# A two-layer decoder on one core: the query and key projections of the last layer issued ahead of the scores in their slots on TensorE

## The reference

```python
q = apply_rotary_interleaved((query @ Wq).reshape(b, t, 2 * H, D), cos, sin)
k = apply_rotary_interleaved((query @ Wk).reshape(b, t, 2 * H, D), cos, sin)
s = jnp.where(mask, jnp.einsum('bthd,bshd->bhts', q, k) * scale, NEG)
a = jax.nn.softmax(s, axis=-1)          # for (q1, k1) and for (q2, k2)
attn_freq = rfft(attn1) - lambda_full * rfft(attn2)   # then a filter, irfft, rms norm, @ Wout
```

## Time and profile before

| | |
|---|---|
| median of 3 runs | 1355.0 us (1351.44 to 1356.1) |
| the profiled execution | 1357.66 us, span in the trace 1355.9 us |
| TensorE busy | 1122.7 us (83%) |
| VectorE busy | 918.3 us (68%) |
| ScalarE busy | 567.1 us (42%) |
| GpSimd busy | 539.5 us (40%) |
| mean granted TensorE clock | 0.915 |

### The profile page before, as it was taken

How to read it: one execution, slowest core, us unless ns; L and a number is a source line. 1 busy time by engine, 2 the same in 40 slices (tenths; PEclk the granted TensorE clock), 3 DMA queues, 4 the chain that set the end, 5 groups by cost and what they waited for, 6 DMA issues and landing times.

```text
span 1355.9 us, 25392 instructions
## 1 busy us (share of the span) xinstructions
PE 1122.7 (83%) x8338; PEld 960.4 (71%) x8338; DVE 918.3 (68%) x2195; ACT 567.1 (42%) x1998; POOL 539.5 (40%) x575
## 2 busy tenths in 40 slices
PE   6999999889899998966686999997588887788753
PEld 6898898888888888855575888885356655555532
DVE  5757778687877778687763557654367688787753
ACT  5533343333433242413242333332187776667631
POOL 1112222333424343343330556667134455563564
PEclk9999999999999999976897999998699898898876
DMA  5410010101010100106564777766200000000000
GB/s 169 133 65 23 1 41 1 61 14 56 18 49 22 39 27 19 47 30 190 157 198 146 144 143 116 116 113 84 70 17 9 24 17 24 16 17 9 16 24 16
DMA packets 72663, 84.13 MB, mean 62 GB/s; under 512 B 11720, under 2 KB 62632, under 8 KB 72408
## 3 DMA queue, kind: packets, MB, share of 16 engines
q1 hardware_dynamic: 55608, 60.74, 15.1%
q0 software_dynamic: 14592, 19.41, 8.5%
q10 hardware_dynamic: 2336, 2.36, 0.5%
HBM read 49.90 MB, written 32.58 MB: 61 GB/s over the span
## 4 chain that ended last, share of the span: by engine, by line
PE 38%; DVE 28%; DMA 12%; issue 9%; ACT 6%; POOL 5%; SPq 2%; DVEq 0%; POOLq 0%; ACTq 0%
PE bank L514 4%; PE bank L1987 4%; PE bank L515 4%; PE bank L516 4%; DMA yt<-y_sb,xe 3%; DMA xs<-xg,slot 3%; PE bank L575 3%; PE bank L1501 3%; DMA x_sh<-y_sb,xe 2%; PE bank L2000 2%; DVE at_lo L924 2%; DVE k_st L2295 2%; ACT ex L2119 2%; DMA xe<-xs 1%; PE bank L563 1%
## 5 line engine op out<-in xcount | busy, mean ns | idle before, releaser
L741 ACT ACTIVATE qk<-bank,b_col 128x256 f32<-128x256 f32 x256 | 107.1, 471 | 220.4 <-PE bank L516 218.0
L2119 ACT ACTIVATE ex<-bank,nmx 128x64 f32<-128x64 f32 x512 | 153.9, 353 | 70.8 <-DVE nmx L2304 63.8
L414 POOL TENSOR_TENSOR probs<-shifted,rowinv 64x512 f32<-64x512 f32 x64 | 71.0, 1109 | 276.4 <-DVE rowinv L912 209.7
L514 PE MATMUL bank<-xt_hi,w_hi 128*128 128x256 f32 x512 | 153.9, 301 | 5.3 <-DVE w_lo L876 4.9
L515 PE MATMUL bank<-xt_lo,w_hi 128*128 128x256 f32 x512 | 147.6, 288 | 0.0
L516 PE MATMUL bank<-xt_hi,w_lo 128*128 128x256 f32 x512 | 147.1, 287 | 0.0
L1885 POOL TENSOR_TENSOR k_bd<-k_st,bd_mask 128x512 f32<-128x512 f32 x64 | 69.7, 1094 | 153.0 <-PE bank L2000 136.2
L2119 ACT ACTIVATION_READ_ACCUMULATOR ex<-bank,nmx 128x1 f32 x512 | 123.0, 247 | 0.0
L757 ACT ACTIVATE at_hi<-bank,b_col 128x256 fp32r<-128x256 f32 x128 | 53.7, 471 | 134.2 <-PE bank L575 134.2
L1557 ACT ACTIVATE act_e<-bank 128x176 f32<-128x176 f32 x112 | 35.5, 317 | 173.4 <-PE bank L1447 173.4
L514 PEld LDWEIGHTS bank<-xt_hi,w_hi 128*128 128x128 f32 x512 | 101.2, 198 | 6.4 <-issue 4.5
(11 more groups left out here) (300 smaller groups left out, 3256.5 us busy)
## 6 DMA issues: line engine op xcount, KB each, us to landing
xe<-xs SPq DMA_DIRECT2D x80, 136.0 KB
e_stage<-w_up SPq DMA_DIRECT2D x18, 352.0 KB
terms<-w_qkv SPq DMA_DIRECT2D x12, 512.0 KB, 4.8
down<-w_down SPq DMA_DIRECT2D x16, 176.0 KB
xs<-zero SPq DMA_DIRECT2D x17, 136.0 KB, 2.5
yt<-zero ACTq DMA_DIRECT2D x1, 2176.0 KB, 8.3
xin<-x SPq DMA_DIRECT2D x8, 256.0 KB, 3.1
terms<-w_o SPq DMA_DIRECT2D x4, 512.0 KB, 4.8
```

Of the source, the lines that this page charges most:

```text
L414: pool.tensor_tensor(probs[r, :, SEQ * s:SEQ * s + SEQ], expd[r, :, :], rowinv[r, :].unsqueeze(2).broadcast_to([SEQ, TC * GH, SEQ]), ALU.m ...
L514: nc.tensor.matmul(out, l_hi, r_hi, start=start, stop=False, skip_group_check=True)
L741: ins = nc.scalar.activation(qk[:, par, hh, o, :], p_proj[hh % 2][:, o * TOK:o * TOK + TOK], ACT.Identity, bias=b_col[:, o, h:h + 1])
L2119: ins = nc.scalar.activation(ex[:, g % 2, j, :], p_s[g % 2][:, j * SEQ:j * SEQ + SEQ], ACT.Exp, bias=nmx[:, g % 2, j:j + 1], accum_out=rs[ ...
```

## The change

In slots 2 to 5 of the periods that prepare a block, `qk(t + 1, u - 2)` is issued between `pv(g - 3)` and `score(g + 2)`; before, it came behind the scores and behind `mix`, `xq_transpose` or `ffn`. Its instructions and its waits are the same, and no other engine's order is edited.

```diff
--- before.py
+++ after.py
@@ -2079,6 +2079,8 @@
                     turn_exp(g - 1)
                 if units(g - 3):
                     pv(g - 3)
+                if blocks(t + 1) and 2 <= u < 6:
+                    qk(t + 1, u - 2)
                 if units(g + 2):
                     score(g + 2)
                 if u == 0 and blocks(t - 2):
@@ -2096,8 +2098,6 @@
                         t1(t + 1)
                     if u == 1:
                         val(t + 1)
-                    if 2 <= u < 6:
-                        qk(t + 1, u - 2)
 
     def scalar_constants(act):
         def constants(r):
```

## The result

The changed kernel is slower: 1376.45 us as the median of 4 runs (1366.55 to 1380.99) beside 1353.22 us for the kernel before (4 runs), ratio 1.0137 with a 95% interval of 1.0094 to 1.018. A second measurement on another occasion gave 1.0148 (1.0109 to 1.0187). The forecast was 1369 in a range of 1357 to 1381.

A forecast was written before the change was run, and what follows sets the result against it. No engine is full; the last layer's period was taken as a ring of waits between engines working strictly in order. Order 8.9 us plus clock 5.1 gave 14 us, bringing the median from 1355.0 to 1369.0, range 1357 to 1381.

The forecast's parts named there:

- Slot 2 and the ring: Slot 2: scores behind qk0, maxima between projection and the rope freeing its bank; rope 2 at 8.25 us, loss 1.43.
- t=0: Period t=0, no rms or mix between: rope 4 at 17.31 us behind qk0, 13.83 before; cost 3.5 us.
- t=1 and 2: Periods t=1 and 2, mix covering the bank's freeing for qk2: rope 4 at 18.47 us; costs 1.9 and 1.5 us.
- the collision of k_st with GpSimd's sum: In t=2 GpSimd's sum moves to about 8.8 us and hits VectorE's k_st writes, giving 0.7 us back.
- the relief of the square: VectorE's rms square no longer runs beside GpSimd's k_bd, 0.69 instead of 1.41 us; 0.7 us taken off.
- rival (c): VectorE's small rms operations, at about 13.0 us, also wait for GpSimd's k_bd; 3 us more, 1372 us; chance 0.10.
- t=3 to 6: Periods t=3 to 6: rope 4 at 18.87 us behind qk0, 18.36 before; cost 0.5 us each, 2.0 for four.
- the lock's bound: VectorE and GpSimd blocking, t=3 to 6: -0.2 us with the square alone, +1.3 with k_st's collision and no relief.
- what delays the fourth rope delays the period: From the fourth rope VectorE is busy up to the period's last maxima, so the rope's delay passes to the period.
- rival (d): Tail of the period: VectorE alternating with GpSimd swallows the shift in t=1 to 6; only t=0 pays 3.5 us; chance 0.14.
- The clock: TensorE's gap before qk0 grows to 2.55 us; clock falls three times of seven at 1.7 us: 5.1 us, bounds 0 to 11.9.
- rival (b): TensorE's clock falls behind qk0's gap in every period: 1355 + 8.9 + 11.9 = 1376 us; chance 0.08.

The follow-up runs named there:

- experiment 3: The changed kernel with nine extra mask matmuls, result overwritten, filling TensorE's gap in front of qk0; ratio 1.0053 to the kernel before.
- experiment 9: The changed kernel with nine mask matmuls in the gap in front of qk0 and five in front of qk3; ratio 1.0037 to the kernel before.
- experiment 1: Against the kernel before, only slot 2's projection (qk0) goes ahead of the scores, slots 3 to 5 as before; ratio 1.0093.
- experiment 6: Against the kernel before, only qk3 moves, from behind the ffn to ahead of it, still behind the scores; ratio 0.9878.

## Why the prediction was right, and where not

**Slot 2 and the ring.** Right. With the clock up, maxima at 3.10 us behind qk0 (forecast 3.12), the first rope at 3.71 (3.72), qk1 at 4.51 (4.53), the second rope at 8.34 (8.25). The second rope is 0.09 us late because VectorE's step from its maxima to it takes 0.72 us and not the 0.60 that the first one takes; why, no row shows.

**t=0.** Forecast +3.5 us and a period of about 35.5; in experiment 3, with qk0's gap filled and the granted clock of the period at 0.95 as before, it is 35.89 us, +3.6, and the fourth rope is at 17.62 us where 17.31 was forecast. Experiment 9 has 35.49 us, but the agreement to the hundredth is chance: its fourth rope is later (17.99) and its clock is up throughout (1.00). In the changed kernel the period was 37.66, since the clock fell behind the gap of qk0.

```profile
1002.66:1038.55 35.89, 30.35 (x233) 21.20 (x238) 20.42 (x49) 25.82 (x141) 9.61 (x11) 0.95 0.03 9
```

**t=1 and 2.** Forecast +1.9 and +1.5, measured +2.9 and +3.5 with the gaps filled. Up to the fourth rope t=1 is right: 17.93 us in experiment 3 against 15.88 before, +2.05 (the fill of experiment 9 adds 0.3). In t=2 it is at 19.02 us where I had 18.47. I let the collision of k_st with GpSimd's sum and the relief of the square cancel; both came, but a small rms operation (`keep`) was locked out too (0.65 against 0.18 us). That was rival (c), of which some 0.5 us per period came in t=2 to 6 and none in t=1. The Trainium skill (SBUF — State Buffer, "Who interferes with whom") names tensor_scalar, which this operation is, among those that can enter a two-port mode and then contend with GpSimd; the trace agrees with these two durations. I had put it at one in ten because no row showed that operation beside k_bd.

The rest lies behind the fourth rope, on TensorE's clock, which my sum priced only in front of qk0. In t=2, behind the maxima that follow the fourth rope, the kernel before has scores and `wout` (line 2048; its result is read by the residual sum on VectorE) at 2.4 GHz, and experiment 9 has the scores and part of `wout` at 1.2 GHz (the second pair of rows):

```profile
1094.88 1.02 PE L2000 MATMUL bank<-k_bd,q_bd 128*128 128x512 f32 x2
1095.73 1.89 PE L2048 MATMUL bank<-wo_w,att_t 128*128 128x256 f32 x8
```

```profile
1103.73 1.92 PE L2000 MATMUL bank<-k_bd,q_bd 128*128 128x512 f32 x2
1105.44 2.33 PE L2048 MATMUL bank<-wo_w,att_t 128*128 128x256 f32 x8
```

That is some 1.3 of the 3.5 us. In t=1 the same group takes 3.53 us instead of 2.93.

**t=3 to 6.** Forecast +0.5 us each from the order, measured -0.7, -1.4 and -1.9 for t=3 to 5 in experiment 9. The fourth rope is within the lock's bound (19.43 instead of 18.87 us behind qk0, 18.37 before). What failed is the step "what delays the fourth rope delays the period": I described the opposite, that the shift is absorbed, as rival (d) for t=1 to 6 and gave it 0.14; it came in the late periods only. It was also my own sign of being wrong, that the periods of t=3 to 6 don't grow though the second rope is late, and for t=4 and 5 it came. In t=4 of experiment 9 the rope is 1.07 us later and the last maxima 1.42 us earlier. Behind the rope VectorE alternates with GpSimd's instructions: k_st takes 1.5 us less and att 0.8 less, of which two later operations take back 0.6. The other 0.7 us is again `wout` on TensorE, 2.28 us instead of 3.02:

```profile
1182.13 3.02 PE L2048 MATMUL bank<-wo_w,att_t 128*128 128x256 f32 x8
```

```profile
1190.88 2.28 PE L2048 MATMUL bank<-wo_w,att_t 128*128 128x256 f32 x8
```

The first of these rows is of the kernel before, the second of experiment 9.

**The clock.** This is the term that was mis-sized. I took three falls of seven, 5.1 us; six of seven came in the trace, and two more at a gap of 1.6 to 1.8 us in front of qk3, a wait on the bank that I didn't price, though my sum had qk3 held until 14.75 us by the bank's read (with the clock up TensorE is done with pv at 13.73 and starts qk3 at 15.31). The fills put the whole at 15 us. The price of one fall in front of qk0 was right: the first rope at 5.3 to 5.4 instead of 3.7 us, 1.7 us, and 1.5 to 2.2 us in a period. A fall at qk3 costs more, 3.3 us in t=2. The 15 us lie above the 11.9 that I gave as the upper bound of this term.

**The sum.** 8.9 + 5.1 was forecast, about 5 + 15 was measured, the 5 with some of the late clock in it: two errors of opposite sign, and a total that came out 4 to 9 us above the forecast. The range held because it took the bound of seven falls in. That the number came so near is in part luck. By the number and by the count of falls the outcome is nearest to rival (b), the clock falling in every period, 1376 us, to which I gave 0.08; but (b) had 8.9 us for the order too, and no fall at qk3.

## What to carry to other kernels

When work is moved into a wait, look at what was already running in that wait. Here the scores ran for nothing while a copy was awaited, and moving a projection ahead of them turned them into path and left the matmul engine idle for 2.55 us instead of 1.37. The order on one engine has to fit the order in which the next engine takes the results. VectorE takes the maxima ahead of the rope, so the scores belong ahead of the projection, and what neither needs (mix, transposes, ffn) behind it: this gains 1.5% (qk3 alone 1.2%), while the projection ahead of the scores costs 1.4%, or nothing if VectorE's order is turned as well.

Price idle gaps on TensorE twice, once for the time and once for the clock behind them, and test the second by filling the gap with matmuls whose result is thrown away. Put the same fill into the kernel before as well, which no experiment here does.

## What the runs showed of the hardware that was not expected

The lower clock doesn't follow from the length of the last gap alone. In the kernel before, none of the seven gaps in front of qk0 (0.98 us in t=0, else 1.37) was followed by slow matmuls; of the seven longer ones (2.06, else 2.55) six were in the changed kernel, and three of the same length in experiment 1; and gaps of 1.58 us in front of qk3 went either way (2.74 us for qk3 in t=3, 1.99 in t=4). Two executions of the changed kernel, on different occasions, fell in the same places: qk0 took 2.89, 3.00, 1.99, 2.80, 2.50, 2.55 and 2.64 us in the second, within 0.03 us of the first. So the falls can repeat from one execution to another. That they always do isn't shown: the fastest of the first four executions, which has no trace, took 1366.55 us with a mean granted clock of 0.925, the profiled one 1380.99 with 0.913.

A small shift of VectorE against GpSimd can be multiplied or absorbed: a fourth rope that came 0.9 us earlier made the period 1.0 us shorter in t=3 and 2.4 in t=4 (experiment 6), and one that came 2.65 us later made it 0.5 us longer (t=4 of the changed kernel). Of the 2.4 us in t=4 of experiment 6, 0.9 is the rope's own shift, and 1.0 more had been added at the second maxima behind it, where k_st took 2.12 instead of 3.65 us and att 1.80 instead of 1.46; the rest comes later in the period.
